# The 1444-key attention's score passes: the two array halves taken in turn in place of one after the other

## The reference

```
qm = split_heads(q @ Wq.T + bq)        # 16 heads of 8
km = split_heads(k @ Wk.T + bk)        # k = v = the context, 1444 keys
vm = split_heads(v @ Wv.T + bv)
scores = einsum('bnlh,bnph->bnlp', qm, km) / sqrt(8)
scores = where(mask, scores, -1e8)
attn = softmax(scores, axis=-1)
out = einsum('bnlp,bnph->bnlh', attn, vm) ... @ Wo.T + bo
```

## Time and profile before

| | us |
|---|---|
| three timed runs, median | 2171.78 (2168.76 to 2175.56) |
| profiled execution, whole | 2172.06 |
| its span, first to last instruction | 2170.3 |
| PE busy / weight loads | 1935.4 / 1224.2 |
| DVE / ACT / POOL busy | 1481.8 / 1321.2 / 670.7 |
| line 1607, 1248 reductions of maxima | 738.6 |
| line 1413, 768 exponentials | 614.9, with 335.4 idle before them |
| line 1512, 3072 score passes | 436.7 |

### The profile page before, as it was taken

One profiled execution on the slowest core, in us unless ns is written; L12 is line 12 of the kernel. 1 busy time (PEld: TensorE's weight loads), 2 busy tenths in 40 slices (PEclk: granted clock), 3 DMA queues, 4 the chain that ended last, 5 costly groups with the idle time before them and its releaser, 6 DMA issues. The chain is left out here.

```text
span 2170.3 us, 42902 instructions
## 1 busy us (share of the span) xinstructions
PE 1935.4 (89%) x16792; PEld 1224.2 (56%) x16792; DVE 1481.8 (68%) x3509; ACT 1321.2 (61%) x2169; POOL 670.7 (31%) x605
## 2 busy tenths in 40 slices
PE   3669999766899999999999999999998899999997
PEld 2536766444465656656566565665655455555553
DVE  4844666785778787777877778777783456577541
ACT  2635677586166666666666666666776345666643
POOL 1410223321422131322313223131221323566576
PEclk9879999877599999999999999999999557999998
DMA  5025555001232332323323232232332102221222
GB/s 157 1 69 189 168 186 172 26 27 47 89 106 82 114 119 72 131 82 114 108 84 131 81 115 97 95 131 68 124 105 75 24 12 45 48 41 36 36 70 42
DMA packets 126293, 190.74 MB, mean 88 GB/s; under 512 B 42018, under 2 KB 99466, under 8 KB 125710
## 3 DMA queue, kind: packets, MB, share of 16 engines
q1 hardware_dynamic: 126094, 188.01, 27.9%
HBM read 104.84 MB, written 11.76 MB: 54 GB/s over the span
## 5 line engine op out<-in xcount | busy, mean ns | idle before, releaser
L1607 DVE TENSOR_REDUCE b_part_max<-psum 128x1 f32<-128x482 f32 (+3 forms) x1248 | 738.6, 650 | 200.8 <-PE psum L1493 186.0
L1413 ACT ACTIVATE b_PT<-psum 128x800 f32<-128x800 f32 x768 | 614.9, 836 | 335.4 <-PE psum L1512 329.5
L1493 PE MATMUL psum<-b_KH,b_QBD 64*128 64x482 f32 (+1 forms) x1152 | 416.2, 441 | 37.4 <-DVE b_part_max L1607 35.0
L1512 PE MATMUL psum<-b_QS,b_KS 64*128 64x200 f32 x3072 | 436.7, 288 | 0.3 <-ACT b_PT L1413 0.3
L1512 PEld LDWEIGHTS psum<-b_QS,b_KS 64*128 64x128 f32 x3072 | 346.2, 187 | 15.2 <-issue 10.5
L1528 PE MATMUL psum<-b_PT,b_V 128*32 128x200 f32 x6144 | 341.4, 339 | 0.3 <-ACT b_PT L1413 0.3
L1493 PEld LDWEIGHTS psum<-b_KH,b_QBD 64*128 64x128 f32 x1152 | 194.1, 189 | 182.1 <-DVE b_part_max L1607 115.7
L1338 POOL TENSOR_TENSOR b_KL<-b_KF,b_KH 128x1444 fp32r<-128x1444 f32 x32 | 106.9, 3340 | 589.7 <-PE psum L1512 566.5
L1528 PEld LDWEIGHTS psum<-b_PT,b_V 128*32 128x32 f32 x6144 | 159.9, 109 | 144.6 <-ACT b_PT L1413 78.7
L1814 POOL TENSOR_TENSOR c_HE<-c_HE,c_G 128x400 f32<-128x400 f32 x128 | 131.5, 1032 | 112.6 <-ACT c_HE L1960 106.0
L426 POOL TENSOR_TENSOR a_rs<-a_ve,a_half 100x4 f32<-100x4 f32 x48 | 48.5, 1011 | 312.6 <-DVE a_ve L918 312.5
(11 more groups left out here) (280 smaller groups left out, 2988.2 us busy)
## 6 DMA issues: line engine op xcount, KB each, us to landing
b_KS<-b_KH SPq DMA_DIRECT2D x64, 722.0 KB
a_CT<-in_ctxt SPq DMA_DIRECT2D x32, 722.0 KB, 5.6
b_CT<-in_ctxt SPq DMA_DIRECT2D x32, 722.0 KB, 4.3
b_KS<-b_KL SPq DMA_DIRECT2D x32, 722.0 KB
a_CN<-in_ctxn SPq DMA_DIRECT2D x32, 704.0 KB
c_G<-gates_scratch SPq DMA_DIRECT2D x16, 800.0 KB, 4.3
att_scratch<-b_AO SPq DMA_DIRECT2D x32, 200.0 KB, 5.8
b_MB<-in_mask SPq DMA_DIRECT2D x32, 180.5 KB, 4.4
```

Of the source, the lines that this page charges most:

```text
L1413: nc.scalar.activation(PT[:, kt % 2, 2 * a:2 * a + 2, :], psum[:, 2 * a:2 * a + 2, 0:TG], ACT.Exp).then_inc(sem["pt_ready"], 1)
L1493: m = mm(bank(b, D, size), QBD[rows, j % 2, tile * D:(tile + 1) * D], KH[rows, j % 2, at_:at_ + size], start=True, stop=True)
L1512: m = mm(bank(p, D, 2 * T, (s % 2) * 2 * T), KS[rows, j % 2, s, kt * D:(kt + 1) * D], QS[rows, j % 2, s * 2 * T:(s + 1) * 2 * T], start=Tr ...
L1607: v.tensor_reduce(part_max[0:rows, q, c:c + 1], bank(b, rows, CHUNKS[c][1]), AX.X, ALU.max)\
```

## The change

The score passes of a tile are put in another order. Before, phases 0 and 1 took half 0's four passes, phases 2 and 3 half 1's. Now every phase `p` takes pass `s = p` of half 0 and then pass `s = p` of half 1. The wait for the exponential goes with each half's first pass, so both such waits stand in phase 0. The signal goes with each half's last pass, so both signals come in phase 3. The passes, their operands, their banks and the number of signals stay the same. Ring jobs keep their phases.

```diff
+SCORE_ORDER = (((0, 0), (1, 0)), ((0, 1), (1, 1)), ((0, 2), (1, 2)), ((0, 3), (1, 3)))
...
             def score_piece(g, j, kt, p):
                 n = g * GROUP + j
-                half, a = divmod(p, 2)
                 if kt == 0 and p == 0:
...
-                if a == 0:
-                    wait(pe, sem["pt_ready"], n * 2 * KT + (2 * kt + half - 1))
-                rows = slice(ROW * half, ROW * half + ROW)
-                for s in (2 * a, 2 * a + 1):
-                    m = mm(bank(p, D, 2 * T, (s % 2) * 2 * T), KS[rows, j % 2, s, kt * D:(kt + 1) * D],
+                for half, s in SCORE_ORDER[p]:
+                    if s == 0:
+                        wait(pe, sem["pt_ready"], n * 2 * KT + (2 * kt + half - 1))
+                    rows = slice(ROW * half, ROW * half + ROW)
+                    m = mm(bank(2 * half + s // 2, D, 2 * T, (s % 2) * 2 * T), KS[rows, j % 2, s, kt * D:(kt + 1) * D],
                            QS[rows, j % 2, s * 2 * T:(s + 1) * 2 * T], start=True, stop=True)
-                if a:
-                    m.then_inc(sem["st_psum"], 1)
+                    if s == PAIRS_ROW - 1:
+                        m.then_inc(sem["st_psum"], 1)
```

## The result

The changed kernel takes 2220.19 us (median of 4 runs, 2216.33 to 2229.02); beside it the kernel before took 2172.74. The ratio is 1.0223, with a 95% interval of 1.0195 to 1.0252, all of it above 1: slower, by 47 us. The forecast was 2224 us, slower. Its profiled span is 2217.8.

A forecast was written before the change was run, and what follows sets the result against it. DVE's reductions and the three-bank ring were taken to set 2.47 us per four-maxima tile. Runs 57.0, first tiles 0.5, tail 6.0 and query tiles -11.6 make +52 on 2172: 2224 us, range 2196 to 2252.

The forecast's parts named there:

- The step from the end to the release: From the end of a tile's score passes, through both exponentials, to PE's next released pass: 0.01 + 1.57 + 0.06 = 1.64 us.
- Held tiles: Tiles waiting for the exponentials' release: 2.68 us with two maxima on half 0, 2.46 with one, 2.24 with none.
- the tail: Tiles after tile 7 of sequence 30, without maxima: 2.24 us each, 35.7 instead of 29.68 in all, so +6.0.
- The run from tile 9 to tile 2: Six tiles, 9, 10, 11, 0, 1 and 2, of each turn of twelve: 16.81 us against 14.91, +1.90 per run.
- Tile 9: Starts unheld; its fourth maximum still waits for DVE, and both exponentials start 1.80 us after its first maximum.
- Tiles 3 to 8: No change: a loop of PE and DVE, with projections or a last maximum between passes, untouched by the pass order.
- Query tiles: Tile 0 in three sequences of four: the query projection costs 0.46 us instead of 1.01; 21 x 0.55 = -11.6.
- The sum: Runs 57.0, tiles 0 to 2 of sequence 0 0.5, tail 6.0, query tiles -11.6: together +52 us on 2172.
- A: Rival: a wait holds only its own half, giving a loop of 2.06 us under the ring's 2.47; stays 2172; chance 0.07.
- B: Rival: passes of the halves run better in turn, saving 0.08 us in each of three steps; 46 less, 2178; chance 0.05.
- C: Rival: steps between passes take 0.19 us for 0.11, about 2.0 more per run, +60, so 2284; chance 0.07.
- D: Rival: PE's standing lowers its granted clock in the run from tile 9 to tile 2; +135, about 2360 us; chance 0.05.

The follow-up runs named there:

- the repeat: The changed kernel run once more, unaltered, beside the same runs of the kernel before: 2214.08 us, ratio 1.0215 (1.0148 to 1.0282).

## Why the prediction was right

- *The step from the end to the release, 1.64.* Measured 991.68 - 990.02 = 1.66 in turn 10. Half the exponential takes 47.8 of the 56.5 us away, so the mechanism is shown, not only fitted.
- *Held tiles.* 2.68 forecast, 2.67 to 2.69 measured; the tail 2.24 and 2.23 to 2.25. Tile 1 takes 2.56 between weighings, but 2.46 between releases (997.04 to 999.50 in the trace), as forecast. The run from tile 9 to tile 2 came to 16.83 for 16.81.
- *Tile 9.* It went as forecast: the fourth maximum still waits for DVE, and both exponentials start behind it at 987.38, 1.86 after the first maximum at 985.52:

```profile
985.52 0.49 PE L1494 MATMUL psum<-b_KH,b_QBD 64*128 64x482 f32 x1
...
986.76 0.48 PE L1494 MATMUL psum<-b_KH,b_QBD 64*128 64x482 f32 x1 [0.22 <-DVE b_part_max L1607]
...
987.38 1.56 ACT L1414 ACTIVATE b_PT<-psum 128x800 f32<-128x800 f32 x2 [1.54 <-PE psum L1512]
```

  Forecast was 1.80. The last pass of half 0 behind the fourth maximum was left out: from that maximum to the exponential it is 0.62, where it was 971.46 - 970.89 = 0.57.
- *Tiles 3 to 8.* Nothing forecast, 0.01 measured.
- *Query tiles.* The projection starts 1.34 after the release at 959.00, as worked out, waiting for DVE; the last two rows are the first maximum of tile 1 and the release after it:

```profile
959.00 0.36 PE L1512 MATMUL psum<-b_QS,b_KS 64*128 64x200 f32 x2 [0.37 <-ACT b_PT L1414]
...
960.34 0.30 PEld L1472 LDWEIGHTS psum<-b_HT,W 128*128 128x128 f32 x2 [0.59 <-DVE b_part_max L1607]
...
961.21 0.50 PEld L1528 LDWEIGHTS psum<-b_PT,b_V 128*32 128x32 f32 x16 [0.57 <-ACT b_PT L1414]
962.03 0.18 PEld L1494 LDWEIGHTS psum<-b_KH,b_QBD 64*128 64x128 f32 x1 [0.32 <-DVE b_QF L1589]
...
964.71 0.29 PEld L1512 LDWEIGHTS psum<-b_QS,b_KS 64*128 64x128 f32 x3 [0.55 <-ACT b_PT L1414]
```

  The term was still mis-sized. A run with one query pass in tile 0 went from 15.90 to 17.40, one without from 14.92 to 16.84: a gain of 0.42 where I had 0.55. Most of the difference is in tile 1, which starts unheld there: 964.71 - 962.03 = 2.68 to the next release, where I had 2.46 and 0.11 for one pass more. Over 21 runs the 0.13 make 2.7 us.
- *The sum.* In stage B +52 forecast, +56.5 measured. Of the 4.5 missing, about 2.7 are the query tiles, 0.6 the run's 1.92 for 1.90, and 1.5 one fall of the clock inside stage B, while the tail cost 0.6 less (+5.4 for +6.0); together that is 4.2. The granted clock was 0.76 in 1459 to 1466, and the run there took 19.59 us where its like take 18.07. The whole time came out 4 us under the forecast because the stretch behind stage B, which I had left as it was, ran at a better clock. So two misses of opposite sign, 4.5 us too little in stage B and 9 too much behind it, partly cancelled: that 2224 came so near to 2220 is in part luck. Stage B is the fairer test, and there 52 stands against 56.5.
- *Rivals.* A (the wait holds only its own half) falls with the two passes that start together at 988.99, behind the second exponential (987.38 + 1.56 = 988.94). B (the halves run better in turn) falls with the measured loss, and with half an exponential there is no gain from turns either: 8.7 us of loss. Tile 8 of the changed kernel has its eight loads within 0.52 us, where half by half they took 0.53:

```profile
1017.84 0.52 PEld L1512 LDWEIGHTS psum<-b_QS,b_KS 64*128 64x128 f32 x8 [0.32 <-issue]
```

  A rule of the Trainium skill stands behind B ("TensorE: Matmul & The Clock Gate", Part 3): a weight load overlaps running matmuls only on other row groups. The changed kernel's trace does not bear it out either, with these 0.52 against 0.53. C (steps of 0.19) falls with 1.03 from release to end. D, a clock that falls in every run, did not come: in the first profile it fell in one run of 30 and cost 1.5 us. In the profile of the repeat it fell in the same run and once more in the tail.

## What to carry to other kernels

Two buffers that one engine fills and another empties worked here because they were out of phase. An order that fills both at the same rate and waits for both at the front keeps every instruction and loses the overlap: the price was the consumer's whole time less what the producer could still do, in every turn that nothing else covered. Read which wait ends last in each kind of turn: here six of twelve tiles paid, the other six were held by something longer and paid nothing. And look at what stands in the queue ahead of a signal: one maximum moved behind it, and with it the ring's wait in turn 9, took back 34 of the 56 us.

## What the runs showed of the hardware that was not expected

- Passes of the two halves did not slow each other: seven passes with three maxima between them end 1.03 us after the release, by the same steps of 0.11 and 0.22 as in a half by itself.
- A maximum and a pass behind it on the same half delayed the change to the weighing by 0.09 us against passes on the other half (0.50 for 0.41).
- With nothing changed, the time of the kernel before spread over 29 us (2153.74 to 2182.93) with its mean granted clock (0.935 to 0.916). A comparison of a few executions can therefore miss or add some 10 us: here the medians gave 47 where stage B grew by 56.5.
